# Layer-0 attention with three transposed slots, nine groups of four transposes to a unit, and one result bank

## The chip, the cores and the metric

The kernel runs on one core of a Trainium2 chip. The metric is the device time of one execution in microseconds (us), as the median of several runs. TensorE (PE) multiplies and transposes into PSUM, which has eight banks of 512 float32 columns on 128 partitions. ScalarE (ACT) and VectorE (DVE) read PSUM; GpSimd (POOL) works on SBUF; SyncE (SP) issues the DMAs.

## The reference, cut to what matters

```python
def _L0_conv_ref(x, sin, cos, mask, ...):          # B, H, W, C = 4, 48, 48, 128; 8 heads of d = 16
    N = H * W                                      # 2304 tokens
    qr = angle_transform(qh, sin, cos).reshape(B, num_heads, N, d)
    kr = angle_transform(kh, sin, cos).reshape(B, num_heads, N, d)
    attn = jnp.einsum('bhnd,bhmd->bhnm', qr, kr) + mask       # mask: one 2304x2304 plane per head
    out = jnp.einsum('bhnm,bhmd->bhnd', jax.nn.softmax(attn, axis=-1), vr)
    ...                                            # + depthwise 5x5 convolution of v, then @ Wo

x = x + _L0_conv_ref(_gn(x), ...)                  # layer 0: the stage that is changed
t = t + _L1_attn_ref(_ln_t(t), ...)                # layer 1: attention, one head of 128
t = t + _L1_ffn_ref(_ln_t(t), ...)                 # layer 1: eight-expert feed-forward
```

## The kernel before

The kernel runs its stages one after the other; the change is in `layer0_core` alone, which computes the softmax attention of layer 0 for 4 images and 8 heads.

**Tiling.** The work goes by pairs of query tiles: 8 heads x 9 pairs = 72 pairs (`ip`). A pair is 256 queries of one head, for all four images. For each image `b` it has two rows `t` (128 queries each), so a pair has 8 rows `r = 2b + t`. A row is 128 queries against 2304 keys, which are 18 key tiles of 128 (`TILES`) or 3 chunks of 768 (`NCH`). Two rows of one image are called a unit here: 4 units to a pair, 288 in all.

**The chain of one row.** (1) `scores` on TensorE, three times, each two matmuls of 384 columns into one of two slots of `Sps` (four banks). (2) `chunk` on VectorE adds the mask, writes the chunk to `S` in SBUF and takes a partial maximum; its `s_taken` frees the `Sps` slot; `row_maximum` joins the three partial maxima. (3) GpSimd computes row maximum minus score over the whole row, in place. (4) `transposes` on TensorE turns 128x128 tiles of `S` into `Tps`, in groups; each group fills a bank. (5) `exp` on ScalarE reads a group from `Tps` and writes it to `PT`; its `exp_done` frees the slot. (6) `values` on TensorE multiplies `PT` by V into `Ops`, with four key tiles in four column groups of the array at once; a half of a pair (two images) has 36 tiles, done in three groups of 12. A float32 matmul of `values` is two instructions in the trace, so a group is x24. (7) `take_o` on ScalarE copies `Ops` to SBUF once for each half of a pair.

**Slots.** `S` has four row slots. `Sps` has two, so the scores with running number n wait for the chunk n - 2. `Tps` has two banks, so the transposes of a group wait for the exponential of the group before the previous one. `Ops` has two banks, one for each half of a pair.

**Order.** TensorE's order is written out by hand in `pair` (L798 and on). For row r: transposes group 0, scores chunk 0 of row r+3, group 1, [a `values` group in rows 0, 1, 2, 4, 5 and 6], group 2, scores chunk 1, group 3, scores chunk 2, group 4. A row's 18 tiles are groups of 4, 4, 4, 4 and 2 (`T_GROUPS`), so ScalarE runs ten exponentials for a unit, eight of 512 columns and two of 256. VectorE adds a tap of a convolution (`conv_tap`, 1.4 us) after rows 2, 5 and 7. Every engine takes its instructions in order, so a wait at the head holds all behind it.

Of the kernel before, what the change touches and what calls it, by code (L numbers as in the profile page):

```python
# [20 lines left out]
P = 128  # L21
# [463 lines left out]
def layer0_core(nc, s, ident, taps, mask):  # L485
# [5 lines left out]
    with ExitStack() as ctx:  # L491
# [14 lines left out]
        Sps = ps("Sps", [P, 2, 2, BANK])  # L506
        Tps = ps("Tps", [P, 2, BANK])
        Ops = ps("Ops", [P, B, 2 * P])

# [19 lines left out]
        V_GROUPS = 2 * TILES // V_TILES  # L529
        T_GROUPS = [range(first, min(first + 4, TILES)) for first in range(0, TILES, 4)]  # L530
        TG = len(T_GROUPS)

        S_SLOTS, T_SLOTS, PT_SLOTS, O_SLOTS = 2, 2, 2, 2
        ROW_SLOTS = 4
# [108 lines left out]
        def _(act):  # L643
# [7 lines left out]

            def exp(ip, b, t):

                for g, tiles in enumerate(T_GROUPS):
                    if t == 0 and g in (0, 3):
                        act.wait_ge(pt_used, V_GROUPS * (B // 2 * ip + b // 2) + (V_GROUPS if b % 2 else 1 + g // 3))
                    act.wait_ge(t_ready, TG * (ROWS * ip + 2 * b + t) + (g + 1 + TG * ROW_SLOTS))
                    act.activation(PT[:, b % 2, tiles.start:tiles.stop, cols(P, t)],  # L658
                                   Tps[:, (t + g) % T_SLOTS, 0:len(tiles) * P].rearrange("p (t q) -> p t q", q=P),
                                   ACT.Exp, scale=-1.0).then_inc(exp_done, 1)  # L660

            def take_o(ip, p, half):

                act.wait_ge(pt_used, V_GROUPS * (B // 2 * ip + half + 1 + 1))
                if half == 0:
                    act.wait_ge(o_stored, 16 * STORES * (ip + 1))
                    alone(act)
                act.activation(O[:, bass.ds(p, 1), cols(2, half), :].rearrange("p a b q -> p (a b) q"), Ops[:, cols(2, half), :],
                               ACT.Copy).then_inc(o_taken, 1)

            def pair(ip, first=False, head=None, next_head=None):

                for b in range(B):
                    exp(ip, b, 0)
                    exp(ip, b, 1)
                    if b == 0 and not first:
                        take_o(ip - 1, (ip - 1) % 2, 1)
                        if head is not None:
                            place_v(head, 1)
                    if b == 2:  # L680
                        take_o(ip, ip % 2, 0)
                        if next_head is not None:
                            place_v(next_head, 0)
# [16 lines left out]
        def _(dve):  # L700
# [32 lines left out]
            def pair(ip, p, start=False):  # L733

                dve.wait_ge(mask_in, 32 * (ip + 1))
                for r in range(ROWS):

                    dve.wait_ge(t_ready, TG * (ROWS * ip + r + 1))
                    chunk(ip, p, r, 0)
# [18 lines left out]
        def _(pe):  # L758
            pe.sem_inc(t_ready, TG * ROW_SLOTS)
            pe.sem_inc(pt_used, V_GROUPS)  # L760
# [14 lines left out]

            def transposes(ip, r, g):
                if g == 0:
                    pe.wait_ge(shifted, ROWS * ip + r + 1)
                pe.wait_ge(exp_done, TG * (ROWS * ip + r) + g + 1)
                for k, kt in enumerate(T_GROUPS[g]):  # L780
                    last = pe.transpose(Tps[:, (r + g) % T_SLOTS, cols(P, k)], S[:, r % ROW_SLOTS, cols(P, kt)], ident[:, :])  # L781
                last.then_inc(t_ready, 1)

            def values(ip, half, group):

                if group == 0:
                    pe.wait_ge(o_taken, 2 * ip + half + 1)
                    pe.wait_ge(v_placed, 2 * (ip // HEAD_PAIRS) + half + 1)
                pe.wait_ge(exp_done, TG * (ROWS * ip + 4 * half + (4 if group else 2)) + T_SLOTS)
                for i in range(V_TILES * group, V_TILES * (group + 1)):  # L790
                    j = i % COLS
                    kt, image = i % TILES, i // TILES
                    b = 2 * half + image
                    last = pe.matmul(Ops[32 * j:32 * (j + 1), b, :], V[:, b * TILES + kt, :], PT[:, image, kt, :],  # L794
                                     start=kt < COLS, stop=kt >= TILES - COLS)
                last.then_inc(pt_used, 1)

            def pair(ip, p, start=False, end=False):  # L798

                for r in range(ROWS):  # L800
                    def ahead(c):
                        if r + LEAD < ROWS:
                            scores(ip, p, r + LEAD, c)
                        elif not end:
                            scores(ip + 1, 1 - p, r + LEAD - ROWS, c)

                    transposes(ip, r, 0)
                    ahead(0)
                    transposes(ip, r, 1)
                    if r in (0, 1) and not start:  # L810
                        values(ip - 1, 1, r + 1)
                    if r in (4, 5):
                        values(ip, 0, r - 3)
                    if r in (2, 6):
                        values(ip, r // 4, 0)
                    transposes(ip, r, 2)
                    ahead(1)
                    transposes(ip, r, 3)
                    ahead(2)
                    transposes(ip, r, 4)  # L820

# [974 lines left out]
```

## Time and profile before

| | |
|---|---|
| median of 3 runs | 4024.16 us (4020.73 to 4025.4) |
| the profiled execution | 4022.89 us, of which the span of the trace is 4020.8 us |
| granted TensorE clock, mean over the span | 0.968 |
| first and last transposes of the changed stage | 255.9 us and 2888.5 us from the start of the span |

Busy times are of each engine, matrix multiplies (PE) apart from loads of the stationary operand (PEld), which overlap them. A matmul's end in the trace is modelled: consecutive rows of PE overlap by some 0.1 to 0.2 us, so distances are taken here from start to start. In the timeline, rows of one kind that follow one another are merged (xcount), and what stands in brackets is idle time ahead of them and what ended it. "issue" means that the trace shows nothing that the engine waited for.

### The profile page before, as it was taken

What the parts mean: (1) busy time and instruction counts of PE and PEld (TensorE: products, weight loads), DVE (VectorE), ACT (ScalarE), POOL (GpSimd) and SP (SyncE); (2) the same over time, 40 slices, a digit from 0 to 9 for tenths busy, and PEclk for the clock granted to TensorE, in tenths of its full rate; (3) what the DMA queues carried; (4) which work ended last, traced back from release to release, by engine and by line L of the source; (5) the groups of instructions that cost most, each with busy time, mean ns of one, the idle gap of its engine ahead of it and who ended that gap; (6) DMA issues with size and microseconds to landing.
All of it is one profiled execution on the core that took longest, in us unless ns stands there. A gap on an engine that the chain in (4) does not pass through costs nothing. (4 is left out here: it accounts for less than half of the span.)

```text
span 4020.8 us, 98829 instructions
## 1 busy us (share of the span) xinstructions
PE 3647.2 (91%) x30782; PEld 2653.1 (66%) x30782; DVE 2767.1 (69%) x6801; ACT 2199.8 (55%) x3949; POOL 1445.0 (36%) x671
## 2 busy tenths in 40 slices
PE   7659999999999999999999999999769999999767
PEld 4436666666666666666666666666548787878655
DVE  6857777777777777777777777777556564644598
ACT  3236666666666666666666666666425444444433
POOL 2434444444444444444444444444310000000123
PEclk8879999999999999999999999999879999999978
DMA  5434124214223322322412421222132020000001
GB/s 160 154 91 117 60 88 116 84 60 122 82 85 83 98 82 89 91 85 82 121 60 85 119 83 61 90 82 84 53 114 75 14 74 14 26 1 0 27 13 36
DMA packets 122409, 307.36 MB, mean 76 GB/s; under 512 B 15609, under 2 KB 85292, under 8 KB 101548
## 3 DMA queue, kind: packets, MB, share of 16 engines
q1 hardware_dynamic: 122284, 305.78, 24.7%
q8 instruction: 67, 1.10, 0.1%
q14 instruction: 58, 0.48, 0.0%
HBM read 251.43 MB, written 54.31 MB: 76 GB/s over the span
## 5 line engine op out<-in xcount | busy, mean ns | idle before, releaser
L658 ACT ACTIVATE c_PT<-c_Tps 128x512 f32<-128x512 f32 (+1 forms) x2880 | 1568.1, 555 | 992.0 <-PE c_Tps L781 980.0
L720 DVE CUSTOM_DVE_ANT_0 c_S<-c_Sps,mask_tiles 128x768 f32<-128x768 f32 x1728 | 1602.8, 955 | 733.0 <-PE c_Sps L772 730.9
L639 POOL TENSOR_SCALAR c_S<-c_S,c_row_max 128x2304 f32<-128x2304 f32 x576 | 1261.5, 2190 | 1380.3 <-DVE c_row_max L731 1380.3
L781 PE MATMUL c_Tps<-ident,c_S 128*128 128x128 f32 x10368 | 1642.5, 278 | 74.4 <-ACT c_PT L658 7.4
L781 PEld LDWEIGHTS c_Tps<-ident,c_S 128*128 128x128 f32 x10368 | 1203.6, 140 | 552.7 <-ACT c_PT L658 235.3
L772 PE MATMUL c_Sps<-c_K,c_Q 96*128 (+1 forms) x3456 | 851.9, 327 | 72.8 <-DMA c_Q<-q_parts 39.7
L794 PE MATMUL c_Ops<-c_PT,c_V 128*32 128x256 f32 x10368 | 648.8, 383 | 0.5 <-ACT c_PT L658 0.5
L794 PEld LDWEIGHTS c_Ops<-c_PT,c_V 128*32 128x32 f32 x10368 | 292.7, 109 | 221.2 <-ACT c_PT L658 48.4
L1217 DVE TENSOR_SCALAR_CACHE_REDUCE l_S<-l_Sps 128x384 f32<-128x384 f32 x432 | 240.1, 557 | 270.9 <-PE l_Sps L1064 242.7
L772 PEld LDWEIGHTS c_Sps<-c_K,c_Q 96*128 96x128 bf16 x3456 | 338.8, 98 | 125.2 <-issue 46.4
L994 ACT ACTIVATE l_PT<-l_Tps 128x384 f32<-128x384 f32 x432 | 196.2, 491 | 395.1 <-PE l_Tps L1085 395.1
L1076 PE MATMUL l_Ops<-l_v,l_PT 128*128 (+1 forms) x2592 | 343.7, 278 | 0.1
L1076 PEld LDWEIGHTS l_Ops<-l_v,l_PT 128*128 128x128 f32 x2592 | 311.8, 192 | 12.1 <-ACT l_PT L994 10.9
L713 DVE SCALAR_TENSOR_TENSOR c_conv<-c_vpad,taps,c_conv (+1 forms) x216 | 306.2, 1417 | 3.0
L1064 PE MATMUL l_Sps<-l_kT,l_q_tile 128*128 (+1 forms) x864 | 291.5, 487 | 7.9 <-issue 5.7
L1064 PEld LDWEIGHTS l_Sps<-l_kT,l_q_tile 128*128 128x128 f32 x864 | 158.8, 190 | 106.8 <-issue 10.2
L1085 PE MATMUL l_Tps<-ident,l_S 128*128 128x128 f32 x1296 | 188.6, 273 | 0.8 <-ACT l_S L986 0.8
L1418 POOL MEMSET e_ones<- 128x128 f32 x1 | 0.2, 204 | 477.4 <-POOLq L841 477.4
L1085 PEld LDWEIGHTS l_Tps<-ident,l_S 128*128 128x128 f32 x1296 | 153.5, 141 | 23.2 <-issue 12.9
L986 ACT ACTIVATE l_S<-l_S,l_neg_max 128x2304 f32<-128x2304 f32 x72 | 158.9, 2207 | 8.7 <-DVE l_neg_max L1220 8.7
L963 POOL TENSOR_TENSOR l_xin<-l_xin,l_bo_all 128x384 f32<-128x384 f32 x24 | 25.4, 1092 | 382.5 <-DMA l_xin<-in_x 382.5
L720 DVE DVE_READ_ACCUMULATOR2_ANT c_part_max<- 128x1 f32 x1728 | 143.0, 83 | 0.0
(209 smaller groups left out, 1911.6 us busy)
## 6 DMA issues: line engine op xcount, KB each, us to landing
mask_tiles<-in_mask SPq DMA_DIRECT2D x144, 1152.0 KB, 7.9
numerators<-c_O SPq DMA_DIRECT2D x288, 64.0 KB
l_num<-numerators SPq DMA_DIRECT2D x8, 2304.0 KB, 8.4
q_parts<-f_parts SPq DMA_DIRECT2D x12, 576.0 KB, 3.4
k_parts<-f_parts SPq DMA_DIRECT2D x12, 576.0 KB
c_Q<-q_parts SPq DMA_DIRECT2D x72, 96.0 KB
c_K<-k_parts SPq DMA_DIRECT2D x8, 864.0 KB, 8.7
c_vpad<-v_padded SPq DMA_DIRECT2D x8, 756.0 KB, 14.7
```

Source lines behind the costliest of these rows:

```text
L639: pool.tensor_scalar(S[:, slot, :], S[:, slot, :], -1.0, row_max[:, slot:slot + 1], ALU.mult, ALU.add).then_inc(shifted, 1)
L658: act.activation(PT[:, b % 2, tiles.start:tiles.stop, cols(P, t)], Tps[:, (t + g) % T_SLOTS, 0:len(tiles) * P].rearrange("p (t q) -> p t q ...
L713: dve.scalar_tensor_tensor(out=dst, in0=window[:, :, 0:W], scalar=taps[:, bass.ds(tap, 1)], in1=dst, op0=ALU.mult, op1=ALU.add).then_inc(c ...
L720: dve.tensor_tensor_reduce(out=S[:, r % ROW_SLOTS, cols(CH, c)].rearrange("p (k n) -> p k n", k=2), in0=Sps[:, n % S_SLOTS, :, 0:GW], in1= ...
L772: last = pe.matmul(Sps[:, n % S_SLOTS, k, 0:GW], Q[:, p, r // 2, cols(P, r % 2)], K[:, bass.ds(start, GW)], start=True, stop=True)
L781: last = pe.transpose(Tps[:, (r + g) % T_SLOTS, cols(P, k)], S[:, r % ROW_SLOTS, cols(P, kt)], ident[:, :])
L794: last = pe.matmul(Ops[32 * j:32 * (j + 1), b, :], V[:, b * TILES + kt, :], PT[:, image, kt, :], start=kt < COLS, stop=kt >= TILES - COLS)
L994: act.activation(PT[:, cols(GB, g), :], Tps[:, g % T_SLOTS, 0:GW].rearrange("p (t q) -> p t q", t=GB), ACT.Copy).then_inc(t_taken, 1)
L1064: pe.matmul(Sps[:, g % S_SLOTS, 0:GW], q_tile[:, t, :], kT[:, bass.ds((b % 2) * N + g * GW, GW)], start=True, stop=True).then_inc(s_ready, 1)
L1076: product = pe.matmul(Ops[:, t, 0:C], PT[:, kt, :], v[:, bass.ds((b % 2) * TILES + kt, 1), :].rearrange("p t c -> p (t c)"), start=kt == 0 ...
L1085: block_t = pe.transpose(Tps[:, g % T_SLOTS, cols(P, k)], S[:, t, cols(P, g * GB + k)], ident[:, :])
L1217: dve.tensor_scalar(S[:, t, cols(GW, g)], Sps[:, g % S_SLOTS, 0:GW], 1.0, None, ALU.mult, ALU.max, accum_out=part_max[:, t, g:g + 1]).then ...
```

## The change

`Tps` gets three banks and `Ops` one, for both halves of a pair. The 36 tiles of a unit are now nine groups of four: four full groups of row t = 0, then one group `SPLIT` with the last two tiles of both rows, then four full groups of row t = 1. ScalarE runs nine exponentials of 512 columns for a unit; that of `SPLIT` has another access pattern. The transposes of group g wait for the exponential of group g - 3. The `SPLIT` group waits for the second row's subtraction between its second and third transposes. `values` group 0 of the next half waits for the only result bank (`O_SLOTS = 1`). In TensorE's order `values` groups 1 and 2 of a half now stand in the even units after transposes 1 and after transposes 7, and group 0 in the odd units after transposes 4; the six scores of a unit stand after transposes 0, 2, 3, 4, 6 and 7 (the last one in an even unit behind a `values` group).

```diff
@@ -504,8 +504,8 @@
         conv = sb("conv", [P, 2, N // 2])
 
         Sps = ps("Sps", [P, 2, 2, BANK])
-        Tps = ps("Tps", [P, 2, BANK])
-        Ops = ps("Ops", [P, B, 2 * P])
+        Tps = ps("Tps", [P, 3, BANK])
+        Ops = ps("Ops", [P, 2, 2 * P])
 
         k_in, v_in, q_in, mask_in = sem("k_in"), sem("v_in"), sem("q_in"), sem("mask_in")
         v_ones, v_placed = sem("v_ones"), sem("v_placed")
@@ -527,10 +527,13 @@
         STORES = COLS + 1
         V_TILES = 3 * COLS
         V_GROUPS = 2 * TILES // V_TILES
-        T_GROUPS = [range(first, min(first + 4, TILES)) for first in range(0, TILES, 4)]
+        FULL = [[(t, kt) for kt in range(first, first + 4)] for t in range(2) for first in range(0, TILES - 2, 4)]
+        SPLIT = [(t, kt) for t in range(2) for kt in range(TILES - 2, TILES)]
+        T_GROUPS = FULL[:4] + [SPLIT] + FULL[4:]
         TG = len(T_GROUPS)
-
-        S_SLOTS, T_SLOTS, PT_SLOTS, O_SLOTS = 2, 2, 2, 2
+        ROW_END = [T_GROUPS.index(SPLIT) + 1, TG]
+
+        S_SLOTS, T_SLOTS, O_SLOTS = 2, 3, 1
         ROW_SLOTS = 4
         LEAD = ROW_SLOTS - 1
 
@@ -649,15 +652,22 @@
                 act.wait_ge(v_in, 16 * (h + 1))
                 act.activation(V[:, images, 0:D], V_next[:, images, :], ACT.Copy).then_inc(v_placed, 1)
 
-            def exp(ip, b, t):
-
-                for g, tiles in enumerate(T_GROUPS):
-                    if t == 0 and g in (0, 3):
-                        act.wait_ge(pt_used, V_GROUPS * (B // 2 * ip + b // 2) + (V_GROUPS if b % 2 else 1 + g // 3))
-                    act.wait_ge(t_ready, TG * (ROWS * ip + 2 * b + t) + (g + 1 + TG * ROW_SLOTS))
-                    act.activation(PT[:, b % 2, tiles.start:tiles.stop, cols(P, t)],
-                                   Tps[:, (t + g) % T_SLOTS, 0:len(tiles) * P].rearrange("p (t q) -> p t q", q=P),
-                                   ACT.Exp, scale=-1.0).then_inc(exp_done, 1)
+            def exp(ip, b):
+
+                for g, group in enumerate(T_GROUPS):
+                    if b % 2 == 0 and g in (0, 3):
+                        act.wait_ge(pt_used, V_GROUPS * (B // 2 * ip + b // 2) + 1 + g // 3)
+                    if b % 2 and g == 0:
+                        act.wait_ge(pt_used, V_GROUPS * (B // 2 * ip + b // 2 + 1))
+                    act.wait_ge(t_ready, TG * (B * ip + b) + (g + 1 + TG * ROW_SLOTS // 2))
+                    if group is SPLIT:
+                        dst = PT[:, b % 2, TILES - 2:TILES, :].rearrange("p k (t q) -> p t k q", t=2)
+                        src = Tps[:, g % T_SLOTS, :].rearrange("p (t k q) -> p t k q", t=2, k=2)
+                    else:
+                        t, first = group[0]
+                        dst = PT[:, b % 2, first:first + 4, cols(P, t)]
+                        src = Tps[:, g % T_SLOTS, :].rearrange("p (k q) -> p k q", q=P)
+                    act.activation(dst, src, ACT.Exp, scale=-1.0).then_inc(exp_done, 1)
 
             def take_o(ip, p, half):
 
@@ -665,14 +675,13 @@
                 if half == 0:
                     act.wait_ge(o_stored, 16 * STORES * (ip + 1))
                     alone(act)
-                act.activation(O[:, bass.ds(p, 1), cols(2, half), :].rearrange("p a b q -> p (a b) q"), Ops[:, cols(2, half), :],
+                act.activation(O[:, bass.ds(p, 1), cols(2, half), :].rearrange("p a b q -> p (a b) q"), Ops[:, :, :],
                                ACT.Copy).then_inc(o_taken, 1)
 
             def pair(ip, first=False, head=None, next_head=None):
 
                 for b in range(B):
-                    exp(ip, b, 0)
-                    exp(ip, b, 1)
+                    exp(ip, b)
                     if b == 0 and not first:
                         take_o(ip - 1, (ip - 1) % 2, 1)
                         if head is not None:
@@ -735,7 +744,7 @@
                 dve.wait_ge(mask_in, 32 * (ip + 1))
                 for r in range(ROWS):
 
-                    dve.wait_ge(t_ready, TG * (ROWS * ip + r + 1))
+                    dve.wait_ge(t_ready, TG * (B * ip + r // 2) + ROW_END[r % 2])
                     chunk(ip, p, r, 0)
                     if r:
                         row_maximum(ip, r - 1)
@@ -756,7 +765,7 @@
 
         @block.tensor
         def _(pe):
-            pe.sem_inc(t_ready, TG * ROW_SLOTS)
+            pe.sem_inc(t_ready, TG * ROW_SLOTS // 2)
             pe.sem_inc(pt_used, V_GROUPS)
             pe.sem_inc(o_taken, O_SLOTS)
 
@@ -773,12 +782,14 @@
                                      start=True, stop=True)
                 last.then_inc(s_ready, 1)
 
-            def transposes(ip, r, g):
+            def transposes(ip, b, g):
                 if g == 0:
-                    pe.wait_ge(shifted, ROWS * ip + r + 1)
-                pe.wait_ge(exp_done, TG * (ROWS * ip + r) + g + 1)
-                for k, kt in enumerate(T_GROUPS[g]):
-                    last = pe.transpose(Tps[:, (r + g) % T_SLOTS, cols(P, k)], S[:, r % ROW_SLOTS, cols(P, kt)], ident[:, :])
+                    pe.wait_ge(shifted, ROWS * ip + 2 * b + 1)
+                pe.wait_ge(exp_done, TG * (B * ip + b) + g + 1)
+                for k, (t, kt) in enumerate(T_GROUPS[g]):
+                    if T_GROUPS[g] is SPLIT and k == 2:
+                        pe.wait_ge(shifted, ROWS * ip + 2 * b + 2)
+                    last = pe.transpose(Tps[:, g % T_SLOTS, cols(P, k)], S[:, (2 * b + t) % ROW_SLOTS, cols(P, kt)], ident[:, :])
                 last.then_inc(t_ready, 1)
 
             def values(ip, half, group):
@@ -786,38 +797,52 @@
                 if group == 0:
                     pe.wait_ge(o_taken, 2 * ip + half + 1)
                     pe.wait_ge(v_placed, 2 * (ip // HEAD_PAIRS) + half + 1)
-                pe.wait_ge(exp_done, TG * (ROWS * ip + 4 * half + (4 if group else 2)) + T_SLOTS)
+                pe.wait_ge(exp_done, TG * (B * ip + 2 * half + (2 if group else 1)) + T_SLOTS)
                 for i in range(V_TILES * group, V_TILES * (group + 1)):
                     j = i % COLS
                     kt, image = i % TILES, i // TILES
                     b = 2 * half + image
-                    last = pe.matmul(Ops[32 * j:32 * (j + 1), b, :], V[:, b * TILES + kt, :], PT[:, image, kt, :],
+                    last = pe.matmul(Ops[32 * j:32 * (j + 1), image, :], V[:, b * TILES + kt, :], PT[:, image, kt, :],
                                      start=kt < COLS, stop=kt >= TILES - COLS)
                 last.then_inc(pt_used, 1)
 
             def pair(ip, p, start=False, end=False):
 
-                for r in range(ROWS):
-                    def ahead(c):
-                        if r + LEAD < ROWS:
-                            scores(ip, p, r + LEAD, c)
+                for b in range(B):
+                    def ahead(i):
+                        r, c = 2 * b + LEAD + i // NCH, i % NCH
+                        if r < ROWS:
+                            scores(ip, p, r, c)
                         elif not end:
-                            scores(ip + 1, 1 - p, r + LEAD - ROWS, c)
-
-                    transposes(ip, r, 0)
+                            scores(ip + 1, 1 - p, r - ROWS, c)
+
+                    def behind(group):
+                        if b:
+                            values(ip, b // 2 - 1, group)
+                        elif not start:
+                            values(ip - 1, 1, group)
+
+                    transposes(ip, b, 0)
                     ahead(0)
-                    transposes(ip, r, 1)
-                    if r in (0, 1) and not start:
-                        values(ip - 1, 1, r + 1)
-                    if r in (4, 5):
-                        values(ip, 0, r - 3)
-                    if r in (2, 6):
-                        values(ip, r // 4, 0)
-                    transposes(ip, r, 2)
+                    transposes(ip, b, 1)
+                    if b % 2 == 0:
+                        behind(1)
+                    transposes(ip, b, 2)
                     ahead(1)
-                    transposes(ip, r, 3)
+                    transposes(ip, b, 3)
                     ahead(2)
-                    transposes(ip, r, 4)
+                    transposes(ip, b, 4)
+                    ahead(3)
+                    if b % 2:
+                        values(ip, b // 2, 0)
+                    transposes(ip, b, 5)
+                    transposes(ip, b, 6)
+                    ahead(4)
+                    transposes(ip, b, 7)
+                    if b % 2 == 0:
+                        behind(2)
+                    ahead(5)
+                    transposes(ip, b, 8)
 
             for r in range(LEAD):
                 for c in range(NCH):
```

## Rows read from the trace of the kernel before

**Rows 1.** Page, part 1: busy time and share of the span, by engine

```profile
PE 3647.2 (91%) x30782; PEld 2653.1 (66%) x30782; DVE 2767.1 (69%) x6801; ACT 2199.8 (55%) x3949; POOL 1445.0 (36%) x671
```

**Rows 2.** Busy time of each engine in a stretch of one pair's length, with clock

```profile
core 0: us, PE busy (x) PEld busy (x) DVE busy (x) ACT busy (x) POOL busy (x), PEclk, DMA share, GB/s
1514.86:1551.43 36.57, 35.14 (x336) 24.79 (x337) 26.69 (x60) 22.69 (x43) 17.53 (x8) 1.00 0.23 78
```

**Rows 3.** Tile view of c_Tps: ns min/median/max, first and last start

```profile
L781 PE MATMUL c_Tps<-ident,c_S x10368: 270/272/476, 256.2 to 2888.6; 128*128 128x128 f32 x200
```

**Rows 4.** Waits in 1514.86 to 1551.43 us: total, times, longest

```profile
ACT c_PT L658 <- PE c_Tps L781: 13.7, 27, 1.4
...
PEld c_Tps L781 <- ACT c_PT L658: 3.7, 12, 0.4
PEld c_Tps L781 <- issue: 2.5, 6, 0.4
```

**Rows 5.** Timeline of PE, start and length in us, 1500 to 1520 us

```profile
1503.46 0.49 PE L772 MATMUL c_Sps<-c_K,c_Q 96*128 x2
1503.79 0.60 PE L781 MATMUL c_Tps<-ident,c_S 128*128 128x128 f32 x4
1504.22 0.49 PE L772 MATMUL c_Sps<-c_K,c_Q 96*128 x2
1504.55 1.18 PE L781 MATMUL c_Tps<-ident,c_S 128*128 128x128 f32 x6
1505.57 0.49 PE L772 MATMUL c_Sps<-c_K,c_Q 96*128 x2
1505.90 0.60 PE L781 MATMUL c_Tps<-ident,c_S 128*128 128x128 f32 x4
1506.43 1.50 PE L794 MATMUL c_Ops<-c_PT,c_V 128*32 128x256 f32 x24
1507.86 0.66 PE L781 MATMUL c_Tps<-ident,c_S 128*128 128x128 f32 x4
1508.35 0.49 PE L772 MATMUL c_Sps<-c_K,c_Q 96*128 x2
...
1518.08 0.50 PE L772 MATMUL c_Sps<-c_K,c_Q 96*128 x2 [0.45 <-DVE c_part_max L720]
```

**Rows 6.** Timeline of PEld, the loads around the same place

```profile
1505.07 0.42 PEld L781 LDWEIGHTS c_Tps<-ident,c_S 128*128 128x128 f32 x4 [0.38 <-ACT c_PT L658]
...
1507.86 0.42 PEld L781 LDWEIGHTS c_Tps<-ident,c_S 128*128 128x128 f32 x4 [0.41 <-issue]
...
1533.28 0.42 PEld L781 LDWEIGHTS c_Tps<-ident,c_S 128*128 128x128 f32 x4 [0.38 <-ACT c_PT L658]
...
1536.74 0.42 PEld L781 LDWEIGHTS c_Tps<-ident,c_S 128*128 128x128 f32 x4 [0.38 <-ACT c_PT L658]
```

**Rows 7.** Timeline of ACT: exponentials (L658) and one result copy (L668)

```profile
1504.42 0.94 ACT L658 ACTIVATE c_PT<-c_Tps 128x512 f32<-128x512 f32 x2 [0.17 <-PE c_Tps L781]
...
1510.15 0.59 ACT L668 ACTIVATE c_O<-c_Ops 128x512 f32 x1
1510.66 0.60 ACT L658 ACTIVATE c_PT<-c_Tps 128x512 f32<-128x512 f32 x1
...
1534.74 1.17 ACT L658 ACTIVATE c_PT<-c_Tps 128x512 f32<-128x512 f32 x2 [0.17 <-PE c_Tps L781]
```

**Rows 8.** Timeline of DVE: chunks (L720) and one tap (L713)

```profile
1504.10 0.96 DVE L720 CUSTOM_DVE_ANT_0 c_S<-c_Sps,mask_tiles 128x768 f32<-128x768 f32 x1 [0.65 <-PE c_Sps L772]
...
1504.98 0.95 DVE L720 CUSTOM_DVE_ANT_0 c_S<-c_Sps,mask_tiles 128x768 f32<-128x768 f32 x1
...
1515.65 1.41 DVE L713 SCALAR_TENSOR_TENSOR c_conv<-c_vpad,taps,c_conv  x1
1516.98 0.95 DVE L720 CUSTOM_DVE_ANT_0 c_S<-c_Sps,mask_tiles 128x768 f32<-128x768 f32 x1
```

## The prediction

> **What bounds the kernel now.** I read the page first: TensorE is busy for 91% of the span, VectorE for 69%, ScalarE for 55% [rows 1]. So TensorE's order decides, unless it waits. The tile view says how long the changed stage is: transposes from 256.2 to 2888.6 us, 2632 us, which is 72 pairs of 36.57 us [rows 3]. A window of just that length shows the granted clock at 1.00, that is 2.4 GHz, and no engine but TensorE near its limit: VectorE 26.7 us, ScalarE 22.7, GpSimd 17.5 of 36.57 [rows 2]. "PE busy 35.14" would leave 1.4 us to win, but the rows of a busy PE overlap, and the list of waits for this pair says more: the loads for transposes waited 12 times for ScalarE, 3.7 us in all, and 6 times, 2.5 us, behind `values` with nothing to wait for [rows 4]. The timeline turns this into a price list.
>
> From start to start [rows 5]: a pair of score matmuls takes TensorE 0.33 us (1503.46 to 1503.79), a group of four transposes 0.43 to 0.44 (1503.79 to 1504.22; I take 0.435). From scores at 1505.57 to scores at 1508.35 there are scores, transposes, a `values` group, transposes: 2.78 - 0.33 - 2 x 0.435 = 1.58 for a `values` group, with the idle 0.41 us behind it [rows 6] in it. A row of 18 transposes, three scores and a `values` group so needs 4.5 x 0.435 + 3 x 0.33 + 1.58 = 4.53 us. It takes 4.89 (1503.46 to 1508.35). The other 0.36 is the wait of group 0 of the next row: it comes right behind the group of two, too short to cover the exponential before it, and ScalarE frees the slot only at 1505.07 [rows 6]. A row without `values` needs 2.95; one takes 3.46 (1533.28 to 1536.74 [rows 6]), and the other some 3.7, since there VectorE is behind with a tap and the scores wait for it (0.45 us idle before 1518.08 [rows 5]). For the pair: 36 x 0.435 + 24 x 0.33 + 6 x 1.58 = 15.66 + 7.92 + 9.48 = 33.06 us of TensorE's own work, 3.51 of waits. 72 x 3.51 = 253 us is all that waits can give back.
>
> **The change, part by part.** It removes no transpose, no score and no `values` work, so the 33.06 stand. What it moves:
>
> *Exponentials.* Nine for ten: a unit has two of 256 columns less and one of 512 more. ScalarE starts them 0.58 apart when they queue (two in 1.17, the second 0.6 long [rows 7]), 36 x 0.58 + 2 x 0.6 = 22.1 us to a pair. That the `SPLIT` form costs as much as the others is unseen; doubled to 1.2 us, ScalarE would still have 24.5 of 34. Nothing is on the path here: zero.
>
> *The third slot.* An exponential starts 0.63 us after the first transpose of its group (1503.79 to 1504.42), and the transposes into the freed slot begin 0.66 after that (1504.42 to 1505.08) [rows 5, 7]. With two slots a group can follow the one before the previous after 1.29 us; two groups of transposes and one of scores make 1.20 and, at a row's end, with its half group, less. With three slots the distance that has to be 1.29 is that of three groups, at least 3 x 0.435 + 0.33 = 1.64. So all 3.5 us of ScalarE waits of a pair should go, if ScalarE has no queue. Where it can have one, I walked it. Transposes 5 and 6 stand together, so exponential 6 starts 0.15 late, 7 is back in step. Behind an even unit comes `take_o`, 0.5 to 0.6 us (1510.15 to 1510.66 [rows 7]): with transposes 8 at 0, exponential 8 starts at 0.63, the copy at 1.21, exponential 0 of the next unit at 1.78, and its slot is free at 2.44; transposes 3 come there at 4 x 0.435 + 2 x 0.33 = 2.40. 0.04 us, nothing.
>
> *The scores, where the stall goes.* They have still only two slots. VectorE begins a chunk 0.64 us after the scores begin (1503.46 to 1504.10), and the next scores into the slot start 1.10 after the chunk (1516.98 to 1518.08): 1.74 us from scores n to scores n + 2 [rows 5, 8]. In the new order scores stand after transposes 2, 3 and 4, and the third of these comes 2 x 0.33 + 2 x 0.435 = 1.53 behind the first. So TensorE waits 0.21 us there, once in each unit, and with it transposes 5 and all behind. 4 x 0.21 = 0.84 us to a pair. By the distance from load to chunk and back instead (the load starts 0.1 us ahead of its matmul) it would be 0.32, 1.28 to a pair: I keep this for the range, as the rows of the matmuls are those that set the pace. In the old order the third scores from here came in the next row, over 2 us behind, and only a tap made a wait. Chunks follow one another at 0.88, and a tap sets the next back by 1.33 (1515.65 to 1516.98 [rows 8]). The taps come after the second of the three scores in two units, and after the last of a unit once. The chunk behind the tap then starts 2.21 us after the chunk of the second scores, at 3.73 from the first scores; the scores that need it are the last of the unit, which come at 1.74 + 0.33 + 1.58 + 2 x 0.435 + 0.33 + 0.435 = 5.29 or later, and the slot is free at 4.83. So taps cost nothing more, and the 0.25 us of before go.
>
> *`values`.* Still six groups for a pair. Group 0 waits for the one result bank. `take_o` ends about 1.8 us after transposes 8 of the even unit, and `values` group 0 comes after five more groups of transposes and four scores, at 0.435 + 2.17 + 1.32 + 0.21 = 4.1: 2.3 us of cover. Groups 1 need all exponentials of the unit before; the last is through at 0.63 + 0.6 + 0.06 = 1.29 and the group comes at 3 x 0.435 + 0.33 = 1.64: cover 0.35. Group 2 is followed by scores, not by transposes, which the trace never shows. If their load needs no idle time, up to 0.41 us is won twice a pair, 59 us in all; if it starts as the transposes do and its matmul 0.11 later, 16 us are lost. I take zero, as the only rows behind `values` have the 0.41. The Trainium skill ("TensorE: Matmul & The Clock Gate", Part 3, The mechanism) says that a load overlaps running matmuls only where their row groups differ. By it the scores' load, which shares rows with `values`, could not slip ahead, and the bound of 59 us would be out; no row before shows this pair.
>
> *GpSimd.* The second row of a unit is wanted in the middle of group 4 instead of at group 5. Counted from the first of the three close scores of the unit before: its maximum is taken after the third's chunk, at worst (tap) at 3.73 + 0.88 = 4.6, and with 0.3 to get going and 2.19 for the subtraction (17.53 / 8 [rows 2]) the row is done at 7.1. It is wanted at 5.29 + 0.33 + 0.435 (the end of that unit), then four groups, three scores and half a group: 6.05 + 2.95 = 9.0. Cover 1.9 us: zero, and if it were gone it would cost what is missing.
>
> **Sum.** Pair: 33.06 + 0.84 = 33.90 for 36.57, so 2.67 us less; 72 x 2.67 = 192 us. The stages ahead and behind are as they were. The profiled execution took 4022.89 us (1.3 under the median of the runs shown, 4024.16), so 4023 - 192 = 3831; against the median 3832. The 33.06 rest on rows of 0.01 us, so 0.005 of a group is 0.18 to a pair, 13 us in all.
>
> **The rivals.**
> (a) *Forecast:* ScalarE's waits go and a small score wait comes. 3832, own range 3800 to 3870 (the low end has a part of the 59 us; the high end has 1.28 for 0.84, which is 32 us more).
> (b) *The new waits are larger than in the walk.* Speaks for it: covers of 0.04 and 0.35 us, and three score groups in a row against a 0.88 chunk. If each unit loses one exponential's step (0.58) besides, 288 x 0.3 to 0.58 is 86 to 167 us: 3918 to 3999. Against it: ScalarE and VectorE have 12 and 7 us free in a pair.
> (c) *Nothing binds.* The score wait does not show: 4023 - 253 = 3770, and down to 3711 with free loads behind `values`. Against it: 1.10 us from chunk to scores was read in a real wait.
> (d) *The result bank decides, slower.* `values` group 0 waits for `take_o`, with transposes 5 and all behind it, twice in a pair. It has to cost 2.67 / 2 = 1.3 us each time to undo the gain, so the copy has to come 2.3 + 1.3 = 3.6 us later than walked, and it would be above 4023. ScalarE's 12 us of slack in a pair speak against it.
> (e) *It does nothing:* if the 0.36 us at a row's end were TensorE's own, the time would stay near 4023. The load row names ScalarE and ends 0.05 us after the exponential; a group of four behind a row in step has no such gap.
>
> **Numbers.** (a) 0.62, (b) 0.21, (c) 0.10, (d) 0.04, (e) 0.03. Predicted 3832. The range reaches from 3785 (part of (c)) to 3925 (the near end of (b)). A measurement tells 0.2%, 8 us, from no change. Faster: (a), (b), (c), 0.93; same 0.03; slower 0.04.
>
> **What would show it.** Right: a pair's length near 33.9 us in the windows; loads for transposes that no longer wait for ScalarE, in the list of waits; 288 waits of scores for VectorE's chunk of about 0.2 to 0.3 us; `c_Tps` exponentials 2592, all of 512 columns at 0.60; VectorE's share up to 79% in the stage. Wrong: waits of `values` for `c_O`, of transposes for ScalarE in the odd units, an exponential of `SPLIT` that is much longer, a clock below 1.00, or gaps behind `values` that are another length when scores follow.

## The result, and the profile after

The changed kernel takes 3838.45 us (median of 4 runs, 3837.97 to 3838.92) against 4023.33 us (4 runs); the ratio is 0.9541, 95% interval 0.9524 to 0.9557. It is 4.6% faster. Forecast was 3832 us, range 3785 to 3925. The profiled execution took 3838.61 us, with a span of 3836.5 us at a mean granted clock of 0.964.

The tile view of `c_Tps` in the kernel after (ns min/median/max, first and last start) answers to [rows 3]:

```profile
L792 PE MATMUL c_Tps<-ident,c_S x10368: 270/272/421, 253.8 to 2701.7; 128*128 128x128 f32 x200
L670 ACT ACTIVATE c_PT<-c_Tps x2592: 589/598/653, 256.3 to 2702.1; 128x512 f32<-128x512 f32 x200
```

The stage is 2447.9 us for 2632.4, so 184.5 us less, and the spans differ by 184.3: all of the gain is in the changed stage. A pair takes 34.00 us for 36.56. The exponentials are 2592, with a median of 0.598 us and none outside 0.589 to 0.653; those of `SPLIT`, the fifth of each unit, have the same median, so its pattern costs ScalarE nothing that shows.

The window of one pair in the kernel after, with the columns of [rows 2]:

```profile
1506.93:1540.93 34.00, 33.75 (x338) 25.16 (x336) 26.95 (x60) 20.98 (x39) 17.57 (x8) 1.00 0.58 132
```

The list of waits of that pair (total, times, longest), which answers to [rows 4]:

```profile
PEld c_Sps L781 <- issue: 2.0, 6, 0.4
PEld c_Tps L792 <- issue: 1.6, 4, 0.4
...
```

The 3.7 us in which transposes waited for ScalarE are gone from the list. In their place scores wait, with "issue" as the reason, 6 times. Two of these stand behind `values`. The other four are one to a unit, and the timeline of PE shows what such a one is:

```profile
1503.08 1.50 PE L805 MATMUL c_Ops<-c_PT,c_V 128*32 128x256 f32 x24
1504.52 0.50 PE L781 MATMUL c_Sps<-c_K,c_Q 96*128 x2
...
1505.72 0.49 PE L781 MATMUL c_Sps<-c_K,c_Q 96*128 x2
1506.05 1.04 PE L792 MATMUL c_Tps<-ident,c_S 128*128 128x128 f32 x8
1506.93 0.49 PE L781 MATMUL c_Sps<-c_K,c_Q 96*128 x2
1507.26 0.60 PE L792 MATMUL c_Tps<-ident,c_S 128*128 128x128 f32 x4
1507.69 0.49 PE L781 MATMUL c_Sps<-c_K,c_Q 96*128 x2
1508.02 0.60 PE L792 MATMUL c_Tps<-ident,c_S 128*128 128x128 f32 x4
1508.67 0.50 PE L781 MATMUL c_Sps<-c_K,c_Q 96*128 x2
1509.11 1.50 PE L805 MATMUL c_Ops<-c_PT,c_V 128*32 128x256 f32 x24
```

The group of transposes at 1507.26 is followed by scores after 0.43 us, that at 1508.02 only after 0.65, with no reason given. But the scores at 1508.67 come 1.74 us after the scores at 1506.93, the last but one. That is the distance that the forecast worked out for a slot to be read by VectorE and freed. The timeline of DVE in the kernel after has the chunk between them:

```profile
1507.56 0.96 DVE L729 CUSTOM_DVE_ANT_0 c_S<-c_Sps,mask_tiles 128x768 f32<-128x768 f32 x1 [0.17 <-PE c_Sps L781]
```

It starts 0.63 after the scores of 1506.93 and 1.11 before those of 1508.67. So the 0.21 us is there, under a name ("issue") that does not tell it.

### The profile page after: what moved, and what is told of

It is laid out like the page before. It is cut to its first block and busy times, and to the rows that moved or that the text cites. A ratio compares the mean times of both kernels' runs of the same rounds, so it can differ in the third digit from the quotient of the medians.

```text
span 3836.5 us, 97899 instructions
## 1 busy us (share of the span) xinstructions
PE 3551.4 (93%) x30782; PEld 2678.6 (70%) x30782; DVE 2785.7 (73%) x6801; ACT 2080.6 (54%) x3661; POOL 1448.0 (38%) x671
## 5 line engine op out<-in xcount | busy, mean ns | idle before, releaser
L670 ACT ACTIVATE c_PT<-c_Tps 128x512 f32<-128x512 f32 x2592 | 1457.6, 602 | 927.4 <-PE c_Tps L792 861.4
L792 PE MATMUL c_Tps<-ident,c_S 128*128 128x128 f32 x10368 | 1457.8, 274 | 4.1 <-ACT c_PT L670 4.1
L792 PEld LDWEIGHTS c_Tps<-ident,c_S 128*128 128x128 f32 x10368 | 1219.7, 140 | 261.1 <-issue 119.1
L781 PEld LDWEIGHTS c_Sps<-c_K,c_Q 96*128 96x128 bf16 x3456 | 325.5, 98 | 209.5 <-issue 136.0
L805 PEld LDWEIGHTS c_Ops<-c_PT,c_V 128*32 128x32 f32 x10368 | 304.6, 109 | 222.4 <-ACT c_PT L670 46.4
L722 DVE SCALAR_TENSOR_TENSOR c_conv<-c_vpad,taps,c_conv (+1 forms) x216 | 320.7, 1485 | 2.3
```

The source lines that it names most:

```text
L670: act.activation(dst, src, ACT.Exp, scale=-1.0).then_inc(exp_done, 1)
L722: dve.scalar_tensor_tensor(out=dst, in0=window[:, :, 0:W], scalar=taps[:, bass.ds(tap, 1)], in1=dst, op0=ALU.mult, op1=ALU.add).then_inc(c ...
L781: last = pe.matmul(Sps[:, n % S_SLOTS, k, 0:GW], Q[:, p, r // 2, cols(P, r % 2)], K[:, bass.ds(start, GW)], start=True, stop=True)
L792: last = pe.transpose(Tps[:, g % T_SLOTS, cols(P, k)], S[:, (2 * b + t) % ROW_SLOTS, cols(P, kt)], ident[:, :])
L805: last = pe.matmul(Ops[32 * j:32 * (j + 1), image, :], V[:, b * TILES + kt, :], PT[:, image, kt, :], start=kt < COLS, stop=kt >= TILES - COLS)
```

## The experiments

Each ran beside the kernel before on one chip, and the ratio is to that. The chips of different rows can differ: the kernel before took 4021.86, 4023.57 and 4023.02 us beside the experiments and 4023.33 beside the changed kernel, so a difference between two rows can be off by some 2 us. Times are medians.

| kernel | us | ratio to before, 95% interval |
|---|---|---|
| one result bank alone | 4021.91 | 0.9999 (0.9989 to 1.0008) |
| two slots, nine groups | 4006.3 | 0.9958 (0.9941 to 0.9974) |
| half group in the middle | 3958.13 | 0.9844 (0.9828 to 0.9861) |
| two slots, copy moved | 3928.27 | 0.9760 (0.9744 to 0.9776) |
| `values` bunched | 3941.65 | 0.9793 (0.9777 to 0.9809) |
| changed kernel | 3838.45 | 0.9541 (0.9524 to 0.9557) |
| `values` of 18 | 3861.03 | 0.9595 (0.9579 to 0.9611) |
| scores spread | 3770.81 | 0.9379 (0.9364 to 0.9395) |
| scores spread, taps 3, 5, 7 | 3776.94 | 0.9388 (0.9373 to 0.9404) |
| scores spread, `values` of 18 | 3797.84 | 0.9441 (0.9425 to 0.9456) |
| scores spread, `values` of 16 and 20 | 3741.35 | 0.9298 (0.9282 to 0.9313) |

### One result bank

```diff
 # the kernel before
-        Ops = ps("Ops", [P, B, 2 * P])
+        Ops = ps("Ops", [P, 2, 2 * P])
 ...
-        S_SLOTS, T_SLOTS, PT_SLOTS, O_SLOTS = 2, 2, 2, 2
+        S_SLOTS, T_SLOTS, PT_SLOTS, O_SLOTS = 2, 2, 2, 1
 ...                                  # take_o reads all of Ops
-                    last = pe.matmul(Ops[32 * j:32 * (j + 1), b, :], V[...], PT[...],
+                    last = pe.matmul(Ops[32 * j:32 * (j + 1), image, :], V[...], PT[...],
```

> The kernel before with one result bank for both halves and nothing else. My theory: before, the result copy ran at 1510.15 for 0.59 us and the values group that would now wait for it started at 1511.32, so there is 0.5 us of cover: no change, 4024 us within 8. Rival (d), the bank decides: the group waits for the copy twice a pair, 0.3 us each or more, 4065 us or above, and the list of waits shows values waiting for the copy.

4021.91 us against 4021.86: nothing. The bank that pays for the third slot was spare, and rival (d) has no ground in this order.

### Two slots with the nine groups

```diff
 # the changed kernel
-        Tps = ps("Tps", [P, 3, BANK])
+        Tps = ps("Tps", [P, 2, BANK])
 ...
-        S_SLOTS, T_SLOTS, O_SLOTS = 2, 3, 1
+        S_SLOTS, T_SLOTS, O_SLOTS = 2, 2, 1
 ...
-    Tps[:, g % T_SLOTS, ...]          # in exp (twice) and in transposes
+    Tps[:, (b + g) % T_SLOTS, ...]
```

> The changed kernel (nine groups, new order, one result bank) with only two transposed slots. My theory: a group must follow the one before the previous after 1.29 us; two groups and one score pair make 1.20, which happens some 8 to 10 times a pair, each costing 0.14 with the slower start: 1.1 to 1.4 us a pair on top, 3920 to 3940 us. So the even groups would be worth about 95 us and the third slot about 90. Rival: the third slot is the whole cause and this falls back to 4000 or above. Second rival: the slot is worth nothing once the groups are even, 3840 to 3850.

4006.3 us. This is a miss of 66 us from the near end of my range, and the first rival, 4000 or above, has the number: with the copy where it stands, even groups and the new order give 16 us, the third slot 168. The timeline of PE in the two-slot kernel shows what I had left out:

```profile
1516.12 1.04 PE L792 MATMUL c_Tps<-ident,c_S 128*128 128x128 f32 x8
1516.99 0.49 PE L781 MATMUL c_Sps<-c_K,c_Q 96*128 x2
1517.41 0.66 PE L792 MATMUL c_Tps<-ident,c_S 128*128 128x128 f32 x4
1518.38 0.66 PE L792 MATMUL c_Tps<-ident,c_S 128*128 128x128 f32 x4 [0.32 <-ACT c_PT L670]
```

and of ACT in the same kernel:

```profile
1516.76 0.60 ACT L670 ACTIVATE c_PT<-c_Tps 128x512 f32<-128x512 f32 x1 [1.71 <-PE c_Tps L792]
1517.25 0.59 ACT L678 ACTIVATE c_O<-c_Ops 128x512 f32 x1
1517.73 1.10 ACT L670 ACTIVATE c_PT<-c_Tps 128x512 f32<-128x512 f32 x2
```

Transposes 1 start at 1517.41 and transposes 2 at 1518.38, 0.97 later and not 0.43. They wait for exponential 0, which stands behind exponential 8 (1516.76) and the result copy (1517.25) and begins at 1517.73; 0.65 later the slot is free. That is 0.54 us for each copy, twice a pair: 72 x 1.08 = 78 us. In the order of before the copy was met by a `values` group (1510.15 [rows 7], and the group at 1511.32); in the new order it stands five groups of transposes ahead of the next one, and two slots are too few to get over it.

### The copy moved

```diff
 # the two-slot kernel
-                    exp(ip, b)
-                    if b == 0 and not first:
-                        take_o(ip - 1, (ip - 1) % 2, 1)
-                    if b == 2:
-                        take_o(ip, ip % 2, 0)
 ...                                        # place_v goes with the copy
+                exp(ip, 0)
+                exp(ip, 1, None if first else copy_late)    # take_o behind exponential 2
+                exp(ip, 2)
+                exp(ip, 3, copy_early)                      # take_o behind exponential 2
```

> The two-slot kernel of before, with the result copy (and the placing of V behind it) moved on ScalarE from the end of an even unit to behind the third exponential of the odd unit, where a values group covers it. My theory for the 168 us that the third slot was worth: half of it is the copy, which with two slots holds the transposes 2 of the odd unit back by 0.54 us, twice a pair (78 us); the rest is about ten waits of 0.06 to 0.15. Then this is 3928 us (3915 to 3945). Rival: the copy has nothing to do with it, 4006 unchanged. Second rival: the copy costs the same wherever it stands, since ScalarE is what binds with two slots, 3990 or above.

3928.27 us, on the number. A pair takes 35.23 us in this kernel, 1.23 more than in the changed one, and the timeline of PE has short waits of transposes:

```profile
1504.30 0.49 PE L787 MATMUL c_Sps<-c_K,c_Q 96*128 x2
1504.72 0.66 PE L798 MATMUL c_Tps<-ident,c_S 128*128 128x128 f32 x4
1505.21 0.49 PE L787 MATMUL c_Sps<-c_K,c_Q 96*128 x2
1505.54 1.18 PE L798 MATMUL c_Tps<-ident,c_S 128*128 128x128 f32 x8
1506.55 0.49 PE L787 MATMUL c_Sps<-c_K,c_Q 96*128 x2
```

Transposes come 0.42 us behind scores for a usual 0.33, and eight of them take 1.01 for 0.87. So the 168 us of the third slot are 78 for the copy and 90 for the many short waits. The 90 are what the expectation of the two-slot kernel gave for all. The other way round, this kernel with two slots is 95 us faster than the one before: half of the whole gain needs no third slot once the copy is moved.

### The half group in another place

```diff
 # the kernel before
-        T_GROUPS = [range(first, min(first + 4, TILES)) for first in range(0, TILES, 4)]
+        T_GROUPS = [range(0, 4), range(4, 8), range(8, 10), range(10, 14), range(14, 18)]
```

> The kernel before, with two slots, two banks and its old order, but a row's groups are 4, 4, 2, 4, 4 tiles, so the group of two stands behind the values group instead of at the row's end. My theory: the wait at the row's end falls from 0.36 to 0.14 us in the six rows with values and stays about the same in the two without: 6 x 0.22 = 1.3 us a pair, 3930 us (3900 to 3970). Rival (e), the row's end is TensorE's own time: no change, 4024. Rival, the slots count and not the place: 4010 or above.

3958.13 us, 64 less where 94 were expected, and clear of both rivals. The timeline of PE in this kernel:

```profile
1503.13 0.49 PE L772 MATMUL c_Sps<-c_K,c_Q 96*128 x2
...
1507.82 0.49 PE L772 MATMUL c_Sps<-c_K,c_Q 96*128 x2
...
1512.50 0.49 PE L772 MATMUL c_Sps<-c_K,c_Q 96*128 x2
...
1516.43 0.49 PE L772 MATMUL c_Sps<-c_K,c_Q 96*128 x2
```

A row with `values` takes 4.69 us for the 4.89 of [rows 5]: the 0.36 at the row's end has become 0.16, where 0.14 was expected, 6 x 0.20 = 1.2 us a pair. The pair is 35.61 us, only 0.95 less. What is missing lies behind the tap: that row without `values` takes 3.93 us (1512.50 to 1516.43) for some 3.7 before, and the row with `values` that follows it takes 4.85; the other row without `values` stays at 3.46. One line of code in the old scheme gave a third of the gain of the whole change.

### Scores spread

```diff
 # the changed kernel
                     transposes(ip, b, 1)
+                    ahead(1)
                     if b % 2 == 0:
                         behind(1)
                     transposes(ip, b, 2)
-                    ahead(1)
                     transposes(ip, b, 3)
```

> The changed kernel with the second scores of a unit one group earlier (after transposes 1 instead of 2), so that no scores follow the ones before the previous in less than 1.97 us. My theory: the four score waits of a pair (0.21 us each) go, 34.0 to 33.1 us a pair, 60 us less: 3778 us (3765 to 3795). Rival: the wait only moves, to the scores after transposes 3 or behind a tap, and the time stays within 10 us of 3838. Rival: VectorE is near its limit and the time gets worse.

3770.81 us, 68 us less. In the timeline of PE the odd units now run without a gap:

```profile
1504.24 0.49 PE L781 MATMUL c_Sps<-c_K,c_Q 96*128 x2
1504.57 0.60 PE L792 MATMUL c_Tps<-ident,c_S 128*128 128x128 f32 x4
1505.01 0.49 PE L781 MATMUL c_Sps<-c_K,c_Q 96*128 x2
1505.34 1.04 PE L792 MATMUL c_Tps<-ident,c_S 128*128 128x128 f32 x8
1506.21 0.49 PE L781 MATMUL c_Sps<-c_K,c_Q 96*128 x2
1506.54 0.60 PE L792 MATMUL c_Tps<-ident,c_S 128*128 128x128 f32 x4
1506.97 0.49 PE L781 MATMUL c_Sps<-c_K,c_Q 96*128 x2
```

The window of one pair in this kernel, with the columns of [rows 2]:

```profile
1501.07:1534.09 33.02, 33.02 (x337) 24.96 (x336) 27.03 (x60) 20.80 (x40) 17.50 (x8) 1.00 0.51 143
```

Over the whole stage the pair is 33.07 us, and the prediction's sum of TensorE's own work was 33.06. So the move took away 0.93 us a pair, for 0.84 in the sum, and left no wait that such a sum can tell.

### `values` bunched

```diff
 # the changed kernel
                     if b % 2 == 0:
                         behind(1)
+                    else:
+                        values(ip, b // 2, 0)
 ...
                     ahead(3)
-                    if b % 2:
-                        values(ip, b // 2, 0)
```

> The changed kernel with values group 0 after transposes 1 of the odd unit instead of after transposes 4, so that a pair's values groups stand three, three and twelve groups of transposes apart in place of six, six and six. My theory: the wait for the result copy is under 0.1 us each, 10 us in all, but in the long stretch without values VectorE cannot make up the tap: one wait of about 1.1 us of the last scores of a unit once a pair, 80 us. 3925 us (3895 to 3950), with the waits under scores and not under values. Rival (d), the single bank is what bites: values wait for the copy 0.5 us or more each, 72 us or more, and scores do not. Rival: the spacing is of no account, 3838.

3941.65 us, 103 us more. The timeline of PE in this kernel has one long wait to a pair, and it is for a chunk:

```profile
1512.77 0.60 PE L792 MATMUL c_Tps<-ident,c_S 128*128 128x128 f32 x4
1514.31 0.50 PE L781 MATMUL c_Sps<-c_K,c_Q 96*128 x2 [0.94 <-DVE c_part_max L729]
...
1525.14 0.60 PE L792 MATMUL c_Tps<-ident,c_S 128*128 128x128 f32 x4
1525.88 1.50 PE L805 MATMUL c_Ops<-c_PT,c_V 128*32 128x256 f32 x24
```

From transposes at 1512.77 to scores 1.54 us pass where 0.43 would do: 1.11 once a pair, 80 us. The `values` group at 1525.88 comes 0.74 after its transposes for a usual 0.53. The timeline of ACT has the result copy ahead of it:

```profile
1525.07 0.59 ACT L678 ACTIVATE c_O<-c_Ops 128x512 f32 x1
```

The exponentials that the group needs are through by then, so I put the 0.21 us down to the copy; the list of waits names only "issue". Twice a pair it is 30 us, 110 in sum for 103. So the even distances of `values` in the changed kernel matter, chiefly as a pause for VectorE, and the single bank begins to bind only here, three groups earlier.

### `values` in groups of 18

```diff
 # the changed kernel (and, in the second run, the one with scores spread)
-        TAP_ROWS = (2, 5, 7)
+        TAP_ROWS = (3, 5, 7)
-        V_TILES = 3 * COLS
+        V_TILES = TILES                  # one group in each unit, after transposes 4
 ...                                      # the waits of exp for PT follow the groups
```

> The changed kernel with two values groups of 18 tiles for a half (one in each unit, after transposes 4) instead of three of 12, and the tap of row 2 moved to row 3 so that a values group follows every tap. My theory: the fixed part of a values group, about 0.41 us, is paid four times a pair and not six: 0.82 us less, 59 us: 3779 us (3765 to 3795), with the score wait of 0.21 in each unit still there. Rival: the longer group starves the other engines and new waits eat it, 3838 or above. Rival: a values group costs by its tiles alone, 3838.

> Both: the second scores after transposes 1 and values groups of 18 tiles with the taps at rows 3, 5 and 7. My theory: both gains add, 3771 - 59 = 3712 us (3700 to 3735), 32.3 us to a pair, VectorE busy 83% of the stage. Rival: with so little slack VectorE becomes the bound behind a tap, 3750 or above.

3861.03 and 3797.84 us: both slower, by 23 and 27, where 59 less was expected. In the second kernel the timeline of PE shows no new wait, the group just costs more:

```profile
1503.38 0.49 PE L779 MATMUL c_Sps<-c_K,c_Q 96*128 x2
1503.80 2.35 PE L803 MATMUL c_Ops<-c_PT,c_V 128*32 128x256 f32 x36
1506.08 1.09 PE L790 MATMUL c_Tps<-ident,c_S 128*128 128x128 f32 x8
1507.01 0.49 PE L779 MATMUL c_Sps<-c_K,c_Q 96*128 x2
```

3.63 us from scores to scores, less 0.33 and 8 transposes at 0.87: 2.43 for 18 tiles, where 12 take 1.58. Four are 9.72 us a pair for six at 9.48, which is 17 of the 27 us. My theory, 0.41 us fixed for a group and all else by the tile, is wrong: four groups of 18 would then cost less than six of 12. Two theories were left, a price by the tile, or by rounds over the four column groups, in which 18 tiles need five.

### 16 and 20 tiles, and the taps alone

```diff
 # the kernel with scores spread and groups of 18
-        V_TILES = TILES
-        V_GROUPS = 2 * TILES // V_TILES
+        V_ENDS = [0, 4 * COLS, 2 * TILES]
+        V_GROUPS = len(V_ENDS) - 1
 ...                                      # the waits of exp for PT follow the groups
-                for i in range(V_TILES * group, V_TILES * (group + 1)):
+                for i in range(V_ENDS[group], V_ENDS[group + 1]):
```

The second run is the kernel with scores spread and groups of 12, with `TAP_ROWS = (3, 5, 7)` and nothing else.

> As the kernel with spread scores and groups of 18, but a half's values are split 16 and 20 tiles. In that kernel a group of 18 took 2.43 us from scores to scores (less the scores and transposes) where a group of 12 takes 1.58. Theory A, rounds over the four column groups: 12 tiles are 3 rounds, 18 are 5 (two of the four columns get five tiles); two rounds are 0.85, so 0.425 a round and 0.30 fixed. Then 16 and 20 tiles are 4 and 5 rounds, 2.00 and 2.43, 8.9 us a pair for 9.7 with groups of 18 and 9.5 with groups of 12: 3735 us (3722 to 3755). Theory B, a price by the tile (0.85 for six tiles, nothing fixed): 16 and 20 cost what 18 and 18 do, 3798 us within 10.

> The kernel with spread scores and groups of 12, and only the tap of row 2 moved to row 3, as in the two kernels with longer values groups. My theory: the tap has room there too (the scores that need the slot behind it come 4.3 us later and it is free after 3.95), so 3771 us within 8, and the 27 us that the groups of 18 lost are theirs. Rival: the place of the tap is what cost them, 3785 or above here.

3741.35 us for 16 and 20 tiles: theory A. The timeline of PE:

```profile
1506.81 0.49 PE L779 MATMUL c_Sps<-c_K,c_Q 96*128 x2
1507.23 1.93 PE L803 MATMUL c_Ops<-c_PT,c_V 128*32 128x256 f32 x32
1509.10 1.09 PE L790 MATMUL c_Tps<-ident,c_S 128*128 128x128 f32 x8
1510.02 0.49 PE L779 MATMUL c_Sps<-c_K,c_Q 96*128 x2
...
1514.74 0.50 PE L779 MATMUL c_Sps<-c_K,c_Q 96*128 x2
1515.16 2.37 PE L803 MATMUL c_Ops<-c_PT,c_V 128*32 128x256 f32 x40
1517.46 1.09 PE L790 MATMUL c_Tps<-ident,c_S 128*128 128x128 f32 x8
1518.39 0.49 PE L779 MATMUL c_Sps<-c_K,c_Q 96*128 x2
```

16 tiles take 3.21 - 1.20 = 2.01 us and 20 take 3.65 - 1.20 = 2.45, for 2.00 and 2.43 forecast, and 20 tiles cost what 18 did. A round is 0.43 us and a group 0.30 besides. The place of the tap alone gave 3776.94 us, 6 more than 3770.81; it explains little of the 27, and between two chips, with 4 executions each, it is near what can be told. The kernel with 16 and 20 tiles is the fastest of the study, 7.0% under the one before and 97 us under the changed one.

## Why the prediction was right, point by point

**TensorE's order decides, and 3.5 us of a pair are waits.** Right: the pair without any wait that could be built with the same work takes 33.02 us; 33.06 was the sum.

**Exponentials cost nothing more.** Right: the median is 0.598 us, for `SPLIT` too.

**The third slot takes the waits for ScalarE.** Right as to what goes: transposes have none left in the pair that was listed. What the walk did not see is how much hangs on it. It found 0.04 us at the copy and called it nothing; with two slots the same place costs 0.54. With the copy where it stands the slot's worth is 168 us, not the 90 that I put down when I first took it away, and the even groups with the new order give 16 by themselves; with the copy moved these are 90 and 95. So the gain cannot be shared out between the parts without naming the copy's place. The even groups and the new order were not run apart from each other, nor three slots with the groups of before.

**A score wait of 0.21 us in each unit.** Right in place, length (1.74 us from scores to scores) and number, once in each unit; taking it away gave 68 us for 60 forecast. The bound by the loads' distances, 0.32, was the wrong one of the two. The sign was named wrongly: the list does not name VectorE's chunk as the reason, but "issue".

**Taps cost nothing more.** Right but for their length: between 1000 and 2600 us the mean tap grew from 1.42 to 1.48 us.

**`values`.** The price of a group, 1.58, stands. Scores behind a group start 1.44 us after it (1503.08 to 1504.52), as transposes do (1.43), so zero was right and the bound of 59 us empty. The timeline of the loads (PEld) in the kernel after shows this place and, last, scores behind transposes:

```profile
1503.08 1.02 PEld L805 LDWEIGHTS c_Ops<-c_PT,c_V 128*32 128x32 f32 x24 [0.17 <-ACT c_PT L670]
1504.51 0.11 PEld L781 LDWEIGHTS c_Sps<-c_K,c_Q 96*128 96x128 bf16 x2 [0.41 <-issue]
...
1505.62 0.21 PEld L781 LDWEIGHTS c_Sps<-c_K,c_Q 96*128 96x128 bf16 x2
```

Behind `values` the scores' load starts with its matmul, 0.41 us after the last load of the group, as the Trainium skill has it ("TensorE: Matmul & The Clock Gate", Part 3, The mechanism: a load overlaps running matmuls only where their row groups differ). As a general rule the trace does not bear that out: the 24 loads of `values` are through in 1.02 us, while its last four matmuls start only 1.10 us behind the first, so most of these loads run beside matmuls of their own rows; and behind transposes, which share their rows too, the scores' load at 1505.62 starts 0.10 us ahead of its matmul at 1505.72, just as the last transpose starts (they are 0.108 us apart). So the rule gave the right answer here and cannot be the whole reason. What I had wrong is the reading of the 0.41 us of idle loads as the fixed price of a group, in the bound and then in an experiment; the fixed part came out at 0.30. The distances of [rows 5] hold it: a group starts 0.53 us after the transposes before it and not 0.435, is followed after 1.43 us where three rounds of 0.43 make 1.29, and the transposes behind it take 0.49; that is 0.10 + 0.14 + 0.055.

**The single bank.** Right: no change alone, and the bunched order shows about where it starts to bind.

**The sum.** 33.90 for 34.00 measured, 192 us for 184.9. Of the 0.10, 0.06 is seen at a pair's border, where scores come 1.04 us after the last ones and not 0.98 (1499.97 to 1501.01 in the timeline of PE after); the rest is in the rounding of the rows.

## What to carry to other kernels

When one engine's order is written by hand, price each instruction by the distance of starts in the trace, then compare every distance that a slot allows with the distance the order gives: that sum came within 0.3% of the pair. The engine that is named in a wait is not always what can be moved: a copy in the queue of the releasing engine, met at a place without cover, was worth 78 us, nearly as much as all the short waits together (90). After such a change look for the next slot loop at once, as the scores' one, of 0.21 us, cost 68 us and went with one moved line.

## What the runs showed of the hardware that I had not expected

- Float32 matmuls in four column groups of the array go by rounds: 12, 16, 18 and 20 tiles took 1.58, 2.01, 2.43 and 2.45 us. The 18 tiles, which are no multiple of four, paid for the round of 20. The starts of single matmuls in the traces show it too: they come in fours, one to each column group, 0.216 us apart, two fours to a round; in the group of 18 the last two tiles start by twos, again 0.216 us apart.
- Idle time of the load queue behind such a group (0.41 us, "issue") is not the price of a group: it is the lead of the loads over the matmuls (24 loads are through in 1.02 us, and the next instruction starts at 1.43). It was the same 0.41 behind 18 tiles. Rounds of 0.43 us leave 0.30 us fixed for a group.
- A convolution tap on VectorE takes 1.42 us as the median of the changed kernel and up to 1.75 elsewhere, as in the kernel with scores spread and groups of 18, where it begins at 1504.13. That the subtraction on GpSimd beside it is the cause was not tried.
